# A graph-network kernel on one core: layer 0's means as three products of high and low parts, its feature gathers moved to the attention layers, and the dense products spread over the sort

## The reference

```
# layer 0: mean over the edges of each source
alpha = x @ wc;  beta = x @ wn
sums   = segment_sum(beta[dst], src)          # per source node
counts = segment_sum(ones, src)
x = layernorm(x + alpha + sums / counts[:, None] + bias)
# layer 1, twice: softmax over the edges of each target
scores = einsum('ehd,ehd->eh', q[tgt], k[src]) ...
# layer 3, at the end: uses edge_attr_128, the rows of 128 features of every edge
```

## Time and profile before

| | us |
|---|---|
| median of three runs | 2711.61 |
| the profiled execution | 2706.75 |
| its span, first to last instruction | 2705.0 |
| PE busy / PE weight loads | 2453.5 / 1914.2 |
| DVE busy | 2075.7 |
| ACT busy | 1663.4 |
| POOL busy | 1034.5 |

### The profile page before, as it was taken

One profiled execution on the slowest core, in us unless ns is written; L12 is line 12 of the kernel. 1 busy time (PEld: TensorE's weight loads), 2 busy tenths in 40 slices (PEclk: granted clock), 3 DMA queues, 4 the chain that ended last, 5 costly groups with the idle time before them and its releaser, 6 DMA issues. The chain is left out here.

```text
span 2705.0 us, 44125 instructions
## 1 busy us (share of the span) xinstructions
PE 2453.5 (91%) x12631; PEld 1914.2 (71%) x12631; DVE 2075.7 (77%) x4118; ACT 1663.4 (61%) x3700; POOL 1034.5 (38%) x1030
## 2 busy tenths in 40 slices
PE   5999799999799999997899998688999999986887
PEld 3677555555487999856799996346777777765766
DVE  8698899998535888835388885566899999966667
ACT  1489888883224777712277773141899999935560
POOL 1777000004103444450045454322777777710211
PEclk9999899999898999998999999899999999988989
DMA  2040000004243444222443432412877777831101
GB/s 91 2 123 3 11 0 0 0 0 140 99 162 95 112 114 114 68 93 90 147 110 102 117 105 62 118 49 97 248 241 236 238 239 237 215 72 51 63 4 43
DMA packets 116592, 278.09 MB, mean 103 GB/s; under 512 B 24039, under 2 KB 38314, under 8 KB 116462
## 3 DMA queue, kind: packets, MB, share of 16 engines
q0 software_dynamic: 51328, 138.78, 18.9%
q1 hardware_dynamic: 65134, 137.65, 16.2%
HBM read 208.80 MB, written 59.43 MB: 99 GB/s over the span
## 5 line engine op out<-in xcount | busy, mean ns | idle before, releaser
L761 POOL DMA_INDIRECT feature_rows<-in_edge_attr,ids x352 | 342.8, 974 | 369.1 <-DMA features_dram<-feature_rows 282.9
L1879 POOL DMA_INDIRECT x_got<-table_dram,src_idx x352 | 375.3, 1066 | 110.0 <-issue 81.7
L1312 DVE TENSOR_TENSOR pt_low<-bank,pt_high 128x640 fp32r<-128x640 f32 x320 | 262.9, 822 | 53.5 <-ACT pt_high L1275 52.2
L713 ACT ACTIVATE hot_rest<-hot_dst,slot_w 128x128 bf16<-128x128 bf16 x864 | 272.9, 399 | 40.7 <-DVE hot_dst L663 40.7
L1275 ACT CAST pt_high<-bank 128x640 fp32r<-128x640 f32 x320 | 219.6, 687 | 115.7 <-PE bank L1226 115.6
L2023 DVE TENSOR_TENSOR msg<-bank,x_got 128x512 f32<-128x512 f32 x352 | 237.0, 684 | 41.9 <-ACT msg_high L1968 15.0
L764 POOL COPY ids<-id_idx 128x32 uint32<-128x32 uint32 (+1 forms) x5 | 1.2, 240 | 651.7 <-DVE id_idx L874 338.6
L1306 DVE CUSTOM_DVE_ANT_0 p<-bank,log_counts 128x1254 f32<-128x1254 f32 x160 | 232.7, 1454 | 14.1 <-PE bank L1209 14.0
L1226 PE MATMUL bank<-ident,p 128*128 128x128 f32 x1600 | 229.0, 275 | 2.3 <-DVE pt_low L1312 2.3
L1267 ACT ACTIVATE p<-p,bound 128x1254 f32<-128x1254 f32 x160 | 215.3, 1346 | 9.0 <-DVE bound L1306 9.0
L1237 PE MATMUL bank<-pt_high,val 128*128 128x256 f32 x800 | 213.1, 301 | 0.9 <-DVE agg_t L1318 0.9
(11 more groups left out here) (417 smaller groups left out, 6331.4 us busy)
## 6 DMA issues: line engine op xcount, KB each, us to landing
features_dram<-feature_rows POOLq DMA_DIRECT2D x88, 256.0 KB, 2.4
edge_got<-features_dram SPq DMA_DIRECT2D x88, 256.0 KB, 4.1
qk_dram<-qk_high SPq DMA_DIRECT2D x16, 640.0 KB, 2.9
qk_dram<-qk_low SPq DMA_DIRECT2D x16, 640.0 KB, 4.2
keys<-qk_dram SPq DMA_DIRECT2D x32, 320.0 KB, 4.7
queries<-qk_dram SPq DMA_DIRECT2D x32, 320.0 KB, 6.7
queries_low<-qk_dram SPq DMA_DIRECT2D x32, 320.0 KB, 8.7
acc_a<-zeros SPq DMA_DIRECT2D x1, 6400.0 KB
```

The source lines that it names most:

```text
L713: last = act.activation(hot_rest[:, u, j, q, :], hot_dst[:, u, :, j], ACT.Copy, scale=k.slot_w[:, 1 + q, bass.ds(tile0 + j, 1)])
L761: pool.indirect_dma_start(out=rows[:, g % 2, j * ED:(j + 1) * ED], out_offset=None, in_=self.a.edge_attr_128, in_offset=bass.IndirectOffse ...
L1312: dve.tensor_tensor(p_low[:, made % 3, :, columns], unit(2 * n + u).rearrange("p (j n) -> p j n", n=P), p_high[:, made % 3, :, columns].bi ...
L1879: pool.indirect_dma_start(out=xg[:, g % XRING, j, :], out_offset=None, in_=k.table_dram, in_offset=bass.IndirectOffsetOnAxis(ap=k.src_idx[ ...
```

## The change

What it does, part by part:

1. `dense_behind`: products 4, 5 and 6 follow the columns 2, 5 and 8, and the products 7 to 19 the columns 15, 22, ..., 99; the transpose of tile numbers follows column 106.
2. ACT copies every `beta` product twice: as float32r (`k.beta`, the high part) and as float32 (`k.beta_whole`).
3. Layer 0's product for s: the counts are split into `count_high` (an ACT copy to float32r) and `count_low` (POOL, the difference), `beta` into `k.beta` and `beta_low` (POOL, the difference, ten tiles of 128x512). PE makes high x high, high x low and low x high, 30 matmuls for each s, in float32r.
4. Layer 0's DVE list: `deg` is summed after the numbers of the edges; `of_source` is made by nine additions instead of one reduction; `above` is made by ACT (Relu with bias -1, then Ln with bias 1).
5. Layer 0 gathers no features. Each attention layer gathers 44 groups: 36 in `attend`, 8 in `finish_layer`.
6. Tiles are placed elsewhere to make room (not shown in full).

```diff
 def dense_behind(column):
 
-    if column < SHOTS:
-        return FIRST_DENSE + column
-    n = FIRST_DENSE + SHOTS - 1 + (column - SHOTS + 1) // 4
-    return n if (column - SHOTS + 1) % 4 == 0 and n <= 2 * NB else None
+    early, apart = SHOTS - 1, 7
+    if column <= early:
+        return FIRST_DENSE + column // 3 if column % 3 == 2 else None
+    n = FIRST_DENSE + early // 3 + (column - early) // apart
+    return n if (column - early) % apart == 0 and n <= 2 * NB else None
...
             def copy_beta(n):
                 act.wait_ge(dense_done, n + 1)
-                act.copy(k.beta[:, n, :], ps_d[:, dense_bank(n), :]).then_inc(beta_copied, 1)
+                act.copy(k.beta[:, n, :], ps_d[:, dense_bank(n), :])
+                act.copy(k.beta_whole[:, n, :], ps_d[:, dense_bank(n), :]).then_inc(beta_copied, 1)
...
-LAYER_GROUPS = 40
-ATTEND_GROUPS = 32
-FIRST_GROUPS = NG - LAYERS * LAYER_GROUPS
-assert FIRST_GROUPS % 2 == 0 and LAYER_GROUPS % 2 == 0 and ATTEND_GROUPS % 2 == 0
-def layer0(nc, k, features):
+LAYER_GROUPS = NG // LAYERS
+ATTEND_GROUPS = LAYER_GROUPS - 8
+assert LAYERS * LAYER_GROUPS == NG and LAYER_GROUPS % 2 == 0 and ATTEND_GROUPS % 2 == 0
+def layer0(nc, k):
...
+    over_turned = r
+    r = Region(nc, k.rec_at, k.beta_end)
...
+    count_high, count_low = over_x1t.take("count_high", [P, 2, NB, P], F32R), over_x1t.take("count_low", [P, 2, NB, P], F32R)
+    first_high = Region(nc, k.acc_end + 4 * ROWS * NP, ARENA_END - 4 * NB * D).take("first_count_high", [P, NB, P], F32R)
...
+    def high_of(s):
+        return first_high[:] if s == 0 else count_high[:, s % 2]
...
+            def beta_rest(b):
+                pool.tensor_tensor(beta_low[b][:], k.beta_whole[:, b, :], k.beta[:, b, :].bitcast(F32), ALU.subtract).then_inc(beta_split, 1)
+
+            for b in range(len(low_early)):
+                beta_rest(b)
             pool.wait_ge(ids_made, 1)
-            features.gather(pool, 0, FIRST_GROUPS, 1)
+            for b in range(len(low_early), NB - len(low_late)):
+                beta_rest(b)
+            pool.wait_ge(at_turned, NB)
+            pool.wait_ge(deg_summed, 1)
+            for b in range(NB - len(low_late), NB):
+                beta_rest(b)
+            for s in range(NB):
+                pool.wait_ge(high_made, s + 1)
+                if s >= 2:
+                    pool.wait_ge(gamma_done, s - 1)
+                pool.tensor_tensor(count_low[:, s % 2], k.acc_c[:, :, s * P:(s + 1) * P], high_of(s).bitcast(F32), ALU.subtract).then_inc(low_made, 1)
...
                     pe.wait_ge(at_copied, NB)
                 if s >= GAMMAS:
                     pe.wait_ge(y_done, s - GAMMAS + 1)
+                to = k.bank[:, s % GAMMAS, :]
+                pe.wait_ge(high_made, s + 1)
                 for b in range(NB):
-                    m = pe.matmul(k.bank[:, s % GAMMAS, :], k.acc_c[:, b, s * P:(s + 1) * P], k.beta[:, b, :], start=(b == 0), stop=(b == NB - 1))
+                    pe.matmul(to, high_of(s)[:, b, :], k.beta[:, b, :], start=(b == 0), stop=False)
+                for b in range(NB):
+                    if s == 0:
+                        pe.wait_ge(beta_split, b + 1)
+                    pe.matmul(to, high_of(s)[:, b, :], beta_low[b][:], start=False, stop=False)
+                pe.wait_ge(low_made, s + 1)
+                for b in range(NB):
+                    m = pe.matmul(to, count_low[:, s % 2, b, :], k.beta[:, b, :], start=False, stop=(b == NB - 1))
                 m.then_inc(gamma_done, 1)
                 if s == COUNTED:
                     pe.wait_ge(sources_summed, 1)
...
         def _(act):
+            def high(s):
+                act.copy(high_of(s), k.acc_c[:, :, s * P:(s + 1) * P]).then_inc(high_made, 1)
+
+            high(0)
+            act.wait_ge(minus_made, 1)
             for s in range(NB):
                 act.wait_ge(at_turned, s + 1)
                 if s >= ROWS:
                     act.wait_ge(at_stored[s % ROWS], 16 * (s // ROWS))
                 act.copy(at_rows[:, s % ROWS, 0:2 * 512].rearrange("p (b n) -> p b n", n=512), k.bank[:, 4 * (s % 2):4 * (s % 2) + 2, :])
                 act.copy(at_rows[:, s % ROWS, 2 * 512:NP], k.bank[:, 4 * (s % 2) + 2, 0:NP - 2 * 512]).then_inc(at_copied, 1)
+            act.wait_ge(deg_summed, 1)
+            high(1)
+            high(2)
             for s in range(NB):
+                if s >= 2:
+                    act.wait_ge(logs_masked, s - 1)
+                act.activation(above[:, s % 2, :], k.acc_c[:, s, :], ACT.Relu, bias=minus_one[:]).then_inc(counts_above, 1)
                 act.wait_ge(counts_above, s + 1)
-                act.activation(above[:, s % 2, :], above[:, s % 2, :], ACT.Ln).then_inc(logs_made, 1)
+                act.activation(above[:, s % 2, :], above[:, s % 2, :], ACT.Ln, bias=1.0).then_inc(logs_made, 1)
+                if s + 3 < NB:
+                    act.wait_ge(gamma_done, s + 2)
+                    act.wait_ge(low_made, s + 2)
+                    high(s + 3)
             act.wait_ge(var_ready, 1)
             act.sqrt(norm.dev[:], norm.var[:]).then_inc(dev_ready, 1)
...
-            dve.tensor_reduce(k.deg[:], k.acc_a[:], axis=AX, op=ALU.add).then_inc(deg_summed, 1)
+            dve.memset(minus_one[:], -1.0).then_inc(minus_made, 1)
...
             dve.tensor_copy(k.id_idx[:], number[:, 2, :]).then_inc(ids_made, 1)
+            dve.tensor_reduce(k.deg[:], k.acc_a[:], axis=AX, op=ALU.add).then_inc(deg_summed, 1)
             dve.wait_ge(ids_made, 1)
 
             dve.wait_ge(at_turned, NB)
             dve.wait_ge(deg_summed, 1)
-            dve.tensor_reduce(of_source[:], k.acc_c[:].rearrange("p b n -> p n b"), axis=AX, op=ALU.add).then_inc(sources_summed, 1)
-
-            def above_one(s):
-                if s >= 2:
-                    dve.wait_ge(logs_masked, s - 1)
-                dve.tensor_scalar(above[:, s % 2, :], k.acc_c[:, s, :], 1.0, None, ALU.max).then_inc(counts_above, 1)
-
+            me.then(dve.tensor_tensor(of_source[:], k.acc_c[:, 0, :], k.acc_c[:, 1, :], ALU.add))
+            for b in range(2, NB):
+                last = dve.tensor_tensor(of_source[:], of_source[:], k.acc_c[:, b, :], ALU.add)
+                if b < NB - 1:
+                    me.then(last)
+            last.then_inc(sources_summed, 1)
...
-            above_one(0)
             dve.wait_ge(sources_counted, 1)
             me.mark(dve.tensor_copy(inv[:, 0:NB - 1], k.bank[:, 7, 0:NB - 1]))
             me.then(dve.tensor_tensor(inv[:, NB - 1:NB], k.bank[:, 7, NB - 1:NB], k.pad_rows[:], ALU.add))
             me.then(dve.reciprocal(inv[:], inv[:]))
             for s in range(NB):
-                if s + 1 < NB:
-                    above_one(s + 1)
                 log_counts(s)
...
-            features.gather(pool, FIRST_GROUPS, ATTEND_GROUPS, 2, l)
+            features.gather(pool, 0, ATTEND_GROUPS, 1, l)
...
-            features.gather(pool, FIRST_GROUPS + ATTEND_GROUPS, LAYER_GROUPS - ATTEND_GROUPS, 3, l)
+            features.gather(pool, ATTEND_GROUPS, LAYER_GROUPS - ATTEND_GROUPS, 2, l)
...
-    k.beta = r.take("beta", [P, NB, D], F32)
+    k.beta = r.take("beta_high", [P, NB, D], F32R)
...
+    k.beta_whole = nc.alloc_sbuf_tensor_at("beta_whole", [P, NB, D], F32, offset=ARENA_END - 4 * NB * D)
```

More of the change, by code:

```diff
@@ L246, in sort_edges @@
     col_part = rings.take("col_part", [P, SHOTS, PARTS, P], F32R)
+    rings.end = is_in_at
+    reached, key_row, of_pair = rings.take("reached", [P, NK3], F32), rings.take("key_row", [1, NPAIR // 2], F32), rings.take("of_pair", [P, 4], F32)
     r = Region(nc, k.acc_end, ARENA_END)
@@ L258, in sort_edges @@
     slot_wb, pe_w = r.take("slot_wb", [P, NT], BF16), r.take("pe_w", [P, NT], F32)
-    of_pair, of_pair_f, key_i = r.take("of_pair", [P, 4], F32), r.take("of_pair_f", [P, 5], F32), r.take("key_i", [P, 2], I32)
+    of_pair_f = r.take("of_pair_f", [P, 5], F32)
     id_col, id_col_i = r.take("id_col", [P, 2], F32), r.take("id_col_i", [P, 3], I32)
-    zeros, reached, key_row = r.take("zeros", [P, 512], F32), r.take("reached", [P, NK3], F32), r.take("key_row", [1, NPAIR // 2], F32)
+    key_i = id_col_i
+    zeros = Region(nc, r.at, ARENA_END - 4 * NB * D).take("zeros", [P, 512], F32)
     r = Region(nc, edges_at, edges_end)
@@ L789, in layer0 @@
     x1t_done, x1t_copied, ids_made = S("x1t_transposed"), S("x1t_copied"), S("ids_made")
+    minus_made = S("minus_one_made")
+    beta_split, high_made, low_made = S("beta_split"), S("count_high_made"), S("count_low_made")
     counts_above, logs_made, logs_masked = S("counts_above"), S("logs_made"), S("logs_masked")
@@ L798, in layer0 @@
     of_source, above = r.take("of_source", [P, NP], F32), r.take("counts_above", [P, 2, NP], F32)
-    features.places(Region(nc, k.rec_at, k.beta_end), "0", FIRST_GROUPS)
-    r = Region(nc, ARENA_END - 4 * 3 * NP, ARENA_END)
+    over_turned = r
+    r = Region(nc, k.rec_at, k.beta_end)
```

(18 more changed lines are left out.)

## The result

The changed kernel takes 2756.8 us (median of 4 runs, 2755.8 to 2759.4) against 2711.9 (2705.0 to 2712.4): a ratio of 1.0176, 95% interval 1.0163 to 1.0189. The forecast was 2725.6 with a range of 2709 to 2742: the sign is right, the size is not. The profiled execution has a span of 2754.1 us, 49.1 more than before, where my sum had 14.0 more; the medians differ by 44.9.

What follows compares the result with a forecast made beforehand. PE was taken to bound the sort's early columns and layer 0's means, ACT most sort columns, POOL's reserve to matter in attend. -12.1 - 11.0 + 36.1 + 1.0 = +14.0 on 2706.75 gave 2720.8, as a median 2725.6; range 2709 to 2742.

Steps and rivals of the forecast that it cites:

- The sort: Sort block: PE done with its columns at 271, the scatters' read-back then the last wait, gain 12.1 us.
- Rival C: Sort: a wait of ACT or DVE for a product starves PE; gain 4 instead of 12.1 us, total 2734; 12%.
- The mechanism of the forecast: In attend POOL's longer list of gathers ends last, with all other engines idle at the barrier; overrun 36.1 us.
- Rival B: In attend the 36 groups of gathers fit, so the barrier costs nothing: -23.1 us, total 2688; 10%.
- D: Start of layer 0's means: POOL is waited for only 1.4 us and PE's clock stays; 5.8 us less, 2720; 16%.
- the overrun is 18.8 + 17.3 = 36.1 us: Both attend blocks: four more groups each, 31.4 us, less POOL's reserve; bounds 28 and 46 us.
- The reserve: POOL's idle time in attend less the last store's landing and 0.3 us of barrier: 12.6 and 14.1 us.
- The pace: In attend four late groups at 7.85 us each, undisturbed by loads of the next head, add 31.4 us.
- Rival E: In attend the tail's groups run at 9.13 us each: +24 us, total 2736; 10%.
- if POOL still idles at the barrier, B is right: Sign at attend's end: POOL idling at the barrier would show that its 36 groups fit and the kernel is faster.
- gain 11.0 us: Layer 0's means: 77.3 us for 88.3, with 5.5 us of waits and 1.7 us of slow clock; bounds 17 and 6.
- I had 1 us for both layers: finish_layer: PE enters after a longer idle, costing 1 us over both layers; bounds -2 and 4.

Runs made afterwards that it cites:

- e15: The changed kernel with two products in layer 0 and eight groups gathered there again, 32 in each attend: 2680.2 us against 2706.7, ratio 0.9900.
- e10: The changed kernel run again without any edit: 2759.8 us against 2709.1 for the kernel before, ratio 1.0175.
- e14: The kernel before with only the new places of the sort's products: 2701.0 us against 2706.7, ratio 0.9978.

## Why the prediction was wrong

**Right.** The sort gained 10.9 us where I had 12.1, and PE's rates while the products last were near the sum: seven columns and a product come 9.03 us apart, behind the products of `beta` 9.85 (I had 0.4 us for the latter, it was 0.8). Timeline of PE, columns after each of four products:
```profile
106.96 6.97 PE L574 MATMUL bank<-row_hot,col_part 125*128 125x352 f32 x35
...
116.81 6.96 PE L574 MATMUL bank<-row_hot,col_part 125*128 125x352 f32 x35
...
126.63 6.17 PE L574 MATMUL bank<-row_hot,col_part 125*128 125x352 f32 x35
...
135.67 4.55 PE L574 MATMUL bank<-row_hot,col_part 125*128 125x352 f32 x25
```
But PE was done with its columns at 275.9 and not at 271: 2.5 us of this lay before the end of the last product (207.9 for 205.4), 2.7 behind it. That so little of it shows is luck, since the read-back would have held the sum up to 277.0 anyway. Rival C (PE starves) is refuted. The mechanism of the forecast holds too: in `attend` POOL comes last and every engine waits for it (e15 with e10). Rival B is refuted, D as well.

**The step that failed: "the overrun is 18.8 + 17.3 = 36.1 us".** It was 28.7 + 26.4 = 55.1. The reserve was too large by a term that was left out, and the time until the last store was too short.
- *The reserve.* I took POOL's idle time of 15.42 us less the landing and "0.3 us of barrier". In that idle time lay a DRAIN of 4.29 us that I hadn't looked for. It cost nothing while DVE was later; with POOL last it is on the path, and is 5.93 us long by then. Behind the last store POOL now idles for 8.04 us, where I had 2.49 + 0.3 = 2.8: 5.2 us in each layer, 10.5 in all. The row of the next block named POOL's idle, but not what POOL did in it; the block's own line would have told.
- *The pace.* I put the four late groups at 7.85 us, "what stretches some is SP's loading of the next head, and behind the 32nd group there is none left". POOL's last store came 36.1 us later after the block's start (35.3 in the second layer), not 31.4: +8.6 us in all. Half of that is the late groups: from the 31st store to the 35th it took 33.2 and 33.9 us (e10: 33.8 and 33.2), 8.4 us a group, +4.3 us. Long after SP's last load of a head (1046 us) the distances between the stores from 1098.26 on are 11.7, 8.0, 7.9, 9.6, 7.9 and 7.9 us. Beside the first SP loads `wo_rows` (1098.19), beside the 9.6 it loads nothing; what stretches that one is open. The other half is that the 31st store came 3.0 and 1.5 us later than before (290.3 and 287.5 us after the block's start). Whether that belongs to the change is not shown: with 32 groups in `attend` it came at 284.9 to 293.5 us in the undisturbed traces of the kernel before, e14 and e15, and in e10, with the change, at 289.7 and 295.3. Rival E's mean pace of 9.13 us was above the late groups', and with its 46 us it was still 9 short, for the DRAIN.

The two bullets come to 19.1 us, the difference between 55.1 and 36.1 is 19.0. The DRAIN alone would have taken the forecast from 2725.6 to 2736, still inside the range; with the late stores, or with the means below, it leaves it. One of the signs was misleading as well: "if POOL still idles at the barrier, B is right". POOL idled there for 8.04 us, its DRAIN in them, and B is wrong.

**The means: "gain 11.0 us" was 3.6** (84.7 us for 88.3 from the first product to the last). The waits at the start were 7.26 us for 5.5, inside the bounds: two `beta_low` and a `count_low` of 4.12 us all met additions. But the clock cost more: 2.1 us behind the waits (4.44 for 2.33), 0.5 in the next ten, and 1.6 in s = 3 behind the narrow products of the counts, where two times ten matmuls took 3.1 us each (PEclk 0.74): 4.2 us, and I had 1.7. I had seen no idling in sight that would bring PE's lower clock; PEclk was 0.50 behind these 7.3 us of waits. The pitch was 0.233 for 0.227 us, 1.8 us over 300 matmuls. My 77.3 and these 1.8 + 2.5 + 1.8 make 83.4 of the 84.7 us. Of the other 1.3 us the first twenty matmuls have 1.1 (5.8 us besides the waits, for 4.7), as two of them stand alone between waits, with 0.51 and 0.80 us.

Here the Trainium skill ("SBUF — State Buffer", section "Who interferes with whom") has the rule by which I chose 5.5 us over 1.4: a VectorE operation with two SBUF inputs contends with GpSimd's reads, a tensor_reduce doesn't. The traces agree in both halves: 2.53 against 1.26 us for a `beta_low`. Its third case, a tensor_scalar that can enter a two-port mode, fits e15: of the three early masks the first, beside POOL's subtractions, took 3.03 us, the others 0.82 and 0.81. Durations in ns (min/median/max):
```profile
L944 DVE TENSOR_SCALAR log_counts<-acc_c x3: 809/822/3033, 627.5 to 631.2; 128x1280 f32<-128x1280 f32 x3
```

**Smaller.** The second `finish_layer` is 3.7 us longer; I had 1 us for both layers. Busy time by stretch, before and after, PEclk behind the busy times:
```profile
1652.00:1662.00 10.00, 9.32 (x33) 6.00 (x34) 0.65 (x1) 3.63 (x5) 7.04 (x9) 0.82 0.47 146
...
1698.00:1710.00 12.00, 12.00 (x35) 6.45 (x34) 0.00 (x0) 2.54 (x5) 6.21 (x8) 1.00 0.42 51
```
```profile
1693.00:1703.00 10.00, 9.19 (x27) 5.86 (x28) 0.51 (x1) 3.63 (x5) 6.95 (x8) 0.59 0.47 147
...
1740.00:1752.00 12.00, 11.17 (x27) 5.96 (x28) 0.78 (x1) 1.90 (x4) 6.15 (x8) 0.86 0.44 54
```
After 27.8 us of idle PE's clock is at 0.59 in the first 10 us, before at 0.82, and some 47 us later at 0.86 instead of 1.00. In e10, with 35.1 us of idle, the block took 90.8 us, in e14 and e15, without it, 87.4 and 87.2. The first `finish_layer` took 89.6 us before and 89.9 after, and there the first 10 us were at 0.55 before and 0.52 after: where the clock was low already, nothing was lost. So the clock is a likely cause; no run changed it alone. The edge matrices lost 1.0 us, and 0.6 in e14 with the sort's change alone.

Sum: my 14.0, attend +19.0, the means +7.4, the second finish_layer +2.7, the sort +1.2, the edge matrices +1.0, the last blocks +4.1 and the rest -0.4 make 49.0; measured 49.1. Without the last blocks, which vary by themselves, it is 45, as the medians' 44.9.

## What to carry to other kernels

The reserve of an engine at a barrier is not its idle time: read what the block's own line records for each engine, above all the DRAIN of one that issues transfers, and subtract it at the length it will have. Don't put added work at the pace of an undisturbed step unless a run shows what stretches the others: the late groups took 8.4 us, between the 7.85 of the best and the mean of 9.13. And ask by how much the list's end moves in repeated traces, here by up to 9 us, before a reserve of 12 us is reckoned in tenths. Before two tiles are split into high and low parts, ask whether one of them is exact already: the third product here cost 23 us of layer 0, and small whole numbers leave it nothing to add.

## What the runs showed of the hardware

- POOL's DRAIN took 3.3 to 5.9 us in `attend` and `finish_layer`, and 0.41 us more for each further group of transfers in its block, measured from 8 to 12 and from 32 to 36 groups.
- Beside DVE's additions with two inputs POOL's subtraction of 512 columns took 2.53 us, beside DVE's reduce with one input 1.26.
- The same kernel took 2709 and 2987 us on one chip, with DVE idle up to 75 us and PE and ACT nearly so while POOL issued scatters; the cause is open. The change, which gives POOL more to do in `attend`, costs 1.8% in the one condition; a kernel nearly like it costs 0 to 0.3% in the other.
